# The output bias of the first attention layer, added to x by a transfer instead of by the Pool engine

## The reference

```python
def _L0_gnn_ref(x, adj, Wq, bq, Wk, bk, Wv, bv, Wo, bo):     # 8 heads of 32
    q = (x @ Wq + bq)...; k = (x @ Wk + bk)...; v = (x @ Wv + bv)...
    scores = einsum(q, k) / sqrt(32) + (1.0 - adj) * -1e9
    out = einsum(softmax(scores), v)
    return out @ Wo + bo
h = relu(layernorm(x));  x = x + _L0_gnn_ref(h, ...)
```

## Time and profile before

| what | value |
|---|---|
| median of 3 runs | 1679.87 us (1679.85 to 1681.96) |
| the profiled execution's own time | 1679.06 us |
| its span, first to last instruction | 1677.2 us |
| busy: PE, DVE, ACT, POOL | 92%, 74%, 60%, 31% |
| mean granted TensorE clock | 0.966 of full speed |
| first layer, iterations 0 to 15 | from about 34 us to 313 us |
| second layer | to about 622 us |
| third and fourth layer | to the end |

### The profile page before, as it was taken

One profiled execution on the slowest core, in us unless ns is written; L12 is line 12 of the kernel. 1 busy time (PEld: TensorE's weight loads), 2 busy tenths in 40 slices (PEclk: granted clock), 3 DMA queues, 4 the chain that ended last, 5 costly groups with the idle time before them and its releaser, 6 DMA issues.

```text
span 1677.2 us, 40854 instructions
## 1 busy us (share of the span) xinstructions
PE 1538.0 (92%) x16248; PEld 1316.6 (78%) x16248; DVE 1244.1 (74%) x2509; ACT 1001.9 (60%) x1794; POOL 515.4 (31%) x626
## 2 busy tenths in 40 slices
PE   3999999999999936787599999999999999999997
PEld 3889998988988826666488888888888888888885
DVE  3778788788999957887657676767767676776766
ACT  3666667676777735666456555555565656556453
POOL 2667776767788862221100010000000000000000
PEclk9999999999999967998799999999999999999999
DMA  8000000022233341000100000000000000000000
GB/s 239 28 3 0 0 0 2 3 53 53 50 66 59 58 84 50 1 0 0 1 1 1 26 1 13 13 0 25 0 13 13 0 25 0 13 13 0 26 0 25
DMA packets 36914, 40.07 MB, mean 24 GB/s; under 512 B 12000, under 2 KB 31968, under 8 KB 36832
## 3 DMA queue, kind: packets, MB, share of 16 engines
q0 software_dynamic: 4608, 16.78, 5.3%
q1 hardware_dynamic: 32224, 22.13, 4.6%
HBM read 13.74 MB, written 8.39 MB: 13 GB/s over the span
## 4 chain that ended last, share of the span: by engine, by line
PE 40%; ACT 6%; DVE 3%; issue 1%; ACTq 0%; DVEq 0%
PE scores L85 24%; PE ring L85 11%; DVE l_rhp_lo L1347 2%; ACT l_rhp_hi L1265 2%; ACT l_z L1258 2%; PE scores L1453 2%; ACT l_tok L1252 1%; ACT l_hu L1262 1%; PE ring L1429 1%; PE ring L1485 1%; PE ring L1403 1%; PE ring L1413 0%; ACT l_hn_a L1237 0%; DVE x L1337 0%; DVE l_w_stage L1316 0%
## 5 line engine op out<-in xcount | busy, mean ns | idle before, releaser
L1212 POOL TENSOR_TENSOR l_var_eps<-l_mean_var,l_eps 128x4 f32<-128x4 f32 x16 | 8.2, 510 | 651.5 <-DVE l_mean_var L1312 651.5
L1347 DVE TENSOR_TENSOR l_rhp_lo<-l_rh,l_rhp_hi 128x1024 fp32r<-128x1024 f32 x48 | 58.8, 1226 | 184.3 <-ACT l_rhp_hi L1265 184.3
L293 POOL TENSOR_TENSOR at_s<-at_s,at_mx 128x512 f32<-128x512 f32 x128 | 137.9, 1100 | 57.1 <-DVE at_mx L487 57.1
L85 PE MATMUL scores<-l_agg_hi,l_w_hi 128*128 128x512 f32 x384 | 152.9, 398 | 0.0
L85 PE MATMUL scores<-l_agg_lo,l_w_hi 128*128 128x512 f32 x384 | 151.6, 395 | 0.0
L85 PE MATMUL scores<-l_agg_hi,l_w_lo 128*128 128x512 f32 x384 | 151.5, 395 | 0.0
L299 POOL TENSOR_TENSOR at_s<-at_s,at_rtotal 128x512 f32<-128x512 f32 x128 | 129.6, 1044 | 35.0 <-DVE at_rtotal L493 34.7
L374 ACT ACTIVATE at_s<-at_s 128x512 f32<-128x512 f32 x128 | 78.3, 643 | 71.9 <-POOL at_s L293 71.9
L482 DVE SCALAR_TENSOR_TENSOR at_s<-scores,at_mask 128x512 f32<-128x512 f32 x128 | 87.2, 681 | 42.1 <-PE scores L591 42.0
L1275 ACT ACTIVATE l_hv<-scores,l_bias 128x512 f32<-128x512 f32 x96 | 66.1, 689 | 85.6 <-PE scores L85 85.6
L387 ACT ACTIVATE at_pT<-ring 128x512 f32<-128x512 f32 x128 | 66.5, 603 | 51.6 <-PE ring L626 51.6
(11 more groups left out here) (232 smaller groups left out, 5021.1 us busy)
## 6 DMA issues: line engine op xcount, KB each, us to landing
x<-at_beta_less_one POOLq DMA_DIRECT2D x16, 512.0 KB, 4.6
x<-at_o POOLq DMA_DIRECT2D x16, 512.0 KB, 6.5
out_x<-x SPq DMA_DIRECT2D x16, 512.0 KB, 2.9
x<-in_x SPq DMA_DIRECT2D x1, 6656.0 KB, 29.3
l_w_stage<-in_L_gnn_w_w SPq DMA_DIRECT2D x3, 512.0 KB, 5.2
x<-in_x SPq DMA_DIRECT2D x1, 1024.0 KB, 10.5
at_stage<-in_L_gnn_w_qkv SPq DMA_DIRECT2D x3, 256.0 KB, 3.1
x<-in_x SPq DMA_DIRECT2D x1, 512.0 KB, 4.0
```

What stands on the lines that cost most here:

```text
L85: last = pe.matmul(out, s, m, start=(begins and n == 0), stop=(ends and n == len(terms) - 1))
L293: pool.tensor_tensor(sr, sr, mx[:, r, :].unsqueeze(2).to_broadcast([P, CT * 2, N]), ALU.subtract).then_inc(s_shifted, 1)
L1347: dve.tensor_tensor(rhp.lo[:], rh[:], f32(rhp.hi[:]), ALU.subtract).then_inc(rh_lo_ready, 1)
```

## The change

Pool's addition becomes a transfer that it issues: 512 KB from a new tile `bias_tiles`, which holds the bias row four times, accumulated into chunk i-1 of x. Pool waits before each one for the one before. The semaphore `x_biased` is now raised by 16 per chunk, when the transfer has landed. The tile is filled at the end of iteration 0 by four DVE additions where there was one; the last raises `bias_ready`.

```diff
+        bias_tiles = sb("bias_tiles", [P, CT, D])
...
-                        xc = x_of(i - 1, lay, 0, CT)
-                        pool.tensor_tensor(xc, xc, out_bias[0][:].unsqueeze(1).to_broadcast([P, CT, D]),
-                                           ALU.add).then_inc(x_biased, 1)
+                        if in_first(i - 2, lay):
+                            pool.wait_ge(x_biased, 16 * (i - 1))
+                        pool.dma_start(x_of(i - 1, lay, 0, CT), bias_tiles[:], accum_op=ALU.add)\
+                            .then_inc(x_biased, 16)
...
-                            dve.wait_ge(x_biased, c + 1)
+                            dve.wait_ge(x_biased, 16 * (c + 1))
...
-                        dve.tensor_tensor(out_bias[0][:], out_bias[0][:], scores[:, 0, 0:D], ALU.add)\
-                            .then_inc(bias_ready, 1)
+                        for t in range(CT):
+                            last = dve.tensor_tensor(bias_tiles[:, t, :], out_bias[0][:], scores[:, 0, 0:D], ALU.add)
+                        last.then_inc(bias_ready, 1)
```

## The result

The changed kernel takes 1688.1 us (median of 10 runs, 1681.2 to 1692.6), the kernel before 1680.6 us beside it. The ratio is 1.004, 95% interval 1.0021 to 1.0058: slower by 0.4%. A second set of ten gives the same ratio, 1.004 (1.0022 to 1.0057). I had said no difference that can be told, 1680.5 us, at most 1683.5.

The account below looks back on a forecast made before the run. PE was taken as the bound, fully busy in the first layer's middle. Terms +1.02 - 0.37 - 0.02 = +0.63 us on 1679.87 gave 1680.5 us; 8-in-10 range 1678.0 to 1683.5.

Parts of the forecast that it names:

- Pool's side: Steady iterations: 2.40 us of Pool removed each, shift of r = 2 at most 0.39 us earlier, worth 0 to PE.
- The transfer's own landing: Lands 4.6 us after issue, needed by `take_out` about 19 us later ("even five times" the landing time); costs nothing.
- The start: End of iteration 0: three more DVE additions delay PE by 3 x 0.34 = +1.02 us, bounds 0.9 to 1.27.
- Iteration 1: Shift of r = 2 no longer waits for Pool's addition, so 0.37 us come back to PE, bounds 0 to 0.43.
- Iteration 14: Same order as iteration 1 after the second layer's weights are split; PE gains 0.02 us.
- the 1679.3: Lower end in us of the forecast's own range: stall at the loop's entry absorbs the delay, no run disturbed.
- "Do these transfers slow the engines? ... Taken: 0": First-layer iterations: no slowing by transfers, judged from iteration 18; bounds minus 0.01 to plus 0.09 us an iteration.
- the stall at the loop's entry: Iteration 3: PE's weight load 1.65 us late on "issue"; taken to follow PE's progress, so it absorbs none of 0.63 us.
- The rival of the falling clock: PE's clock falls in iteration 1 after a longer standstill, adding 4.5 us, to 1685.0 us; chance 0.06.

Follow-up runs that it names:

- e5: Kernel before, additions kept, plus one 512 KB dummy transfer per first-layer iteration into a tile nothing reads; ratio 1.0054.
- e8: Changed kernel with the transfer moved to the head of Pool's iteration and the tile filled by ACT after one DVE addition; ratio 0.9998.
- e9: Changed kernel with ACT filling the tile and the transfer issued later, behind the shift of r = 3; ratio 1.0007.
- e14: Second set of the kernel of e8, transfer at the head of Pool's iteration and ACT's fill; ratio 0.9989.
- e4: Changed kernel without any transfer: four DVE additions fill the tile and Pool adds out of it in every iteration; ratio 1.0004.
- e6: Kernel before with eight idle DVE additions ahead of the bias row's, a plain delay without transfer; ratio 1.0027.
- e7: Changed kernel with a cheap start: DVE adds once, ACT copies the row into the tile, transfer in its place; ratio 1.0034.
- e11: The changed kernel again with no edit, a single run for a third trace; took 1693.6 us.

## Why the prediction was wrong

The sum for what I had costed was right, held against the first trace of before. Pool's side: hidden, periods unchanged, the shift of r = 2 released by DVE. The transfer's own landing: hidden. The start: +1.02 us predicted, +0.99 measured on PE's wait. Iteration 1: -0.37 predicted, 0.37 measured. Iteration 14: nothing. Together +0.63, and this is what separates 69.52 from 70.44 at iteration 2 apart from the 0.3 us by which the execution itself began later. In part this agreement is luck: against the second trace of before, whose iteration 0 is 1.06 us longer, the same two iterations come out 0.35 us shorter. Three slips in the working changed nothing: 17.14 against 17.13 us gives a lower bound of +0.01, not -0.01; 19 us hold four landings of 4.6 us, not five; and no sum on record gives the 1679.3.

The step that failed is "Do these transfers slow the engines? ... Taken: 0". I bounded it by the steady iterations, where PE's instructions come out of a loop and, by the DMA view of the kernel before, no packet of queue q8 is under way from about 119 to 260 us. The one place where it mattered was on my list: the stall at the loop's entry. I asked whether that stall could absorb the delay and did not ask what it waits for, nor what the change would put in front of it. In the kernel before Pool's addition in iteration 3 begins at 92.0 and the block at 94.2. In the changed kernel the transfer was issued at 92.92, its data packets began 1.5 us later, and all but the three late ones took 2.7 us: put in the addition's place they cover 93.5 to 96.2, and the block's 94.2 lies within. The timelines and the DMA view of before show the first two times, and transfers of the same form in its second layer could have given the others. What was right was that the stall follows PE's own progress: in the eleven traces without the collision the block begins 7.3 to 7.9 us behind the scores. The collision makes iteration 3 of the changed kernel 2.66 to 3.03 us longer; it is shown by adding only the transfer (e5), by moving it either way (e8, e9, e14) and by taking it away (e4).

The rival of the falling clock was the right kind at the wrong place. A fall can follow when PE's waits lengthen, but in iteration 1 a wait of 1.6 us did not bring it (it did at 3.25 us in e6), while 2.4 us in iteration 3 did, and cost 1.6 us where I had priced 4.5 for a longer stretch (in e7 the same 2.4 us brought none). Its chance of 0.06 was too low, because I looked at one standstill only.

The second failure is the spread. I read three runs as a range of 2 us; 111 runs of the same kernel lie between 1671.5 and 1687.5. A forecast to within 0.2% was finer than the kernel's own runs.

What stays open: of the mean of +6.1 us (standard error 0.8) start and iteration 3 explain 3.3 to 3.7 against the first trace of before. From the scores of iteration 0 to those of iteration 16 the three traces of the changed kernel take 282.90 to 283.16 us, the two of before 279.60 and 280.93, so the whole first layer is worth 2.0 to 3.6. The rest, 2.5 to 4 us, is not located. Behind the scores of iteration 31 the changed kernel's traces take 1097.2 to 1105.1 us and those of before 1098.3 both times, a spread wider than what is looked for. The mean granted clock of the changed kernel's runs is 0.9637 against 0.9651, and over the runs of either kernel a thousandth of it goes with about 1.1 us, some 1.5 us in all. But the fall in iteration 3, half clock for 3.4 of 1684 us, is a thousandth by itself, so most of this is counted already. The traces show further falls in iterations 14, 20 and 31 and in the third layer, but in both kernels, and too few of them to tell their frequency. The kernel with the cheap start but the transfer in its place (e7) is at +5.9 us (standard error 1.2), though its trace has neither the 1.0 us at the start nor the fall in iteration 3. Likewise the early transfer with DVE's fill is 4.4 us slower in the mean than with ACT's fill (20 and 24 runs, standard error 1.1), where PE's longer wait is 1.0 us; and e4, with the fill alone, is at +1.4 (standard error 0.9). I have no cause for the difference.

## What to carry to other kernels

A transfer that its consumer does not wait for can still cost, through what else the DMA engines carry: look in the profile for stalls of the bound engine on "issue" and for packets of the instruction queue, at the entry of a loop (here iteration 3) and in unrolled iterations (here 15), and keep large transfers out of the few microseconds ahead of them. Moving the transfer by 4 to 6 us in Pool's list took the effect out of iteration 3 here; but look at every block again after the move, since the earlier place met one in iteration 15. And before a change of 0.1% is forecast, ask for the spread of the runs: where the clock falls in places that differ from run to run, ten runs tell 0.2% at best.

## What the runs showed of the hardware

Blocks of 16 KB came on a queue of their own, each one packet of 0.9 to 1.5 us in the kernel before, over the same 16 DMA engines as a 512 KB transfer's 128 data packets of 4 KB. Beside such a transfer the block of iteration 3 began 1.6 us later (9.1 instead of 7.5 us behind the scores) and PE's stall was 1.1 us longer; in all 16 traces PE went on 1.3 to 1.5 us after the block's end. Behind a standstill of 2.4 us on "issue" (2.7 in e11) PE's granted clock stood at half (1.2 GHz) for about 3.4 us in four traces, and stayed at full (2.4 GHz) in a fifth (e7) behind the same 2.4 us.
